# One block for the last three stages, and the ternary weights prepared beside the routed steps

## The reference, cut to what matters

```python
x = x + xattn0(ctx, layernorm(x))       # y * silu(layernorm(x))
x = x + moe0(layernorm(x))              # shared + sum of 4 weighted experts
x = x + xattn1(ctx, layernorm(x))       # y * silu(layernorm(x))
x = x + ffn1(layernorm(x))

def quant_weight(w):
    scale = mean(abs(w)) + 1e-5
    return clip(round(w / scale), -1, 1), scale
def quant_act(x):
    s = max(abs(x), -1) / 127 + 1e-5
    return clip(round(x / s), -128, 127), s
# ffn1: q(silu(q(x) @ wg) * (q(x) @ wu)) @ wd, each product times both scales
```

## Time and profile before

| what | us |
|---|---|
| time, median of 3 (2215.13 to 2220.52) | 2215.22 |
| the profiled execution's own time | 2215.32 |
| its span, first to last instruction | 2213.5 |
| tanh of the last routed slot | 1825.42 |
| first gather of `combine` | 1842.26 |
| first matmul of `quant_ffn` | 2018.26 |

### The profile page before, as it was taken

The page is one execution under the profiler, slowest core; times in us unless marked ns, Lnnn a source line. Parts: engine busy times, 40 slices in busy tenths (PEclk is TensorE's granted clock), DMA queues, the critical chain, the costliest instruction groups (busy, mean ns, idle before and its releaser), DMA issues. The chain is left out here.

```text
span 2213.5 us, 27156 instructions
## 1 busy us (share of the span) xinstructions
PE 1629.5 (74%) x8480; PEld 944.7 (43%) x8502; DVE 1754.3 (79%) x2275; ACT 1160.7 (52%) x1773; POOL 1339.9 (61%) x648
## 2 busy tenths in 40 slices
PE   4475666756638558889888889999999990016998
PEld 1122222212217545666566556665556660003554
DVE  2999999999955847997799758887488885856886
ACT  5676776666633025443544365554555550734776
POOL 2679878789952003995399518886168883752111
PEclk7787988889976579999999999999999995557999
DMA  7546546356442820001000333444434227640000
GB/s 264 192 144 212 178 160 213 128 193 203 171 153 77 161 74 6 11 11 39 10 11 1 127 131 118 167 158 162 156 115 166 79 76 307 178 152 6 20 25 29
DMA packets 127144, 264.63 MB, mean 120 GB/s; under 512 B 44546, under 2 KB 48386, under 8 KB 121794
## 3 DMA queue, kind: packets, MB, share of 16 engines
q1 hardware_dynamic: 93890, 184.24, 24.7%
q0 software_dynamic: 11520, 37.76, 5.7%
q10 hardware_dynamic: 21600, 40.90, 5.0%
HBM read 180.41 MB, written 82.44 MB: 119 GB/s over the span
## 5 line engine op out<-in xcount | busy, mean ns | idle before, releaser
L483 POOL TENSOR_TENSOR ssm_hs<-ssm_hs,ssm_Cs 128x1024 f32<-128x1024 f32 x128 | 314.1, 2463 | 88.3 <-DVE ssm_hs L450 88.3
L483 POOL TENSOR_TENSOR moe_hs<-moe_hs,moe_Cs 128x1024 f32<-128x1024 f32 x128 | 301.5, 2356 | 54.7 <-DVE moe_hs L450 53.6
L450 DVE TENSOR_TENSOR_SCAN moe_hs<-moe_dA,moe_bu 128x1024 f32<-128x1024 f32 x128 | 292.5, 2285 | 21.2 <-ACT moe_dA L364 12.7
L473 POOL TENSOR_TENSOR moe_U<-moe_U,moe_hs 128x1024 f32<-128x1024 f32 x128 | 301.8, 2358 | 6.4
L450 DVE TENSOR_TENSOR_SCAN ssm_hs<-ssm_dA,ssm_bu 128x1024 f32<-128x1024 f32 x128 | 291.6, 2279 | 0.1
L296 PE MATMUL ssm_pY<-ssm_hs,ssm_ident 128*128 128x512 f32 x512 | 272.3, 659 | 4.2 <-POOL ssm_hs L483 4.2
L1246 PE MATMUL moe_pgu<-moe_xsh,all_Wreg 128*128 128x256 f16 x1408 | 248.5, 275 | 1.1 <-DVE moe_hsl L1483 0.8
L1296 PE MATMUL moe_pgu<-all_Wreg,moe_xth 128*128 x1280 | 243.6, 313 | 0.0
L706 POOL TENSOR_TENSOR ssm_wlo<-ssm_wst,ssm_whi 128x1360 f16<-128x1360 f32 x64 | 190.4, 2975 | 44.3 <-ACT ssm_wst L642 44.3
L364 ACT ACTIVATE ssm_dA<-ssm_dlt,ssm_A 128x511 f32<-128x511 f32 x256 | 167.9, 709 | 63.8 <-DVE ssm_hs L450 60.9
L1246 PE MATMUL moe_pgu<-moe_xsl,all_Wreg 128*128 128x256 f16 x704 | 193.7, 275 | 0.0
(11 more groups left out here) (248 smaller groups left out, 3471.9 us busy)
## 6 DMA issues: line engine op xcount, KB each, us to landing
ssm_wst<-in_w_all SPq DMA_DIRECT2D x64, 680.0 KB, 4.9
w_hi<-ssm_whi SPq DMA_DIRECT2D x64, 340.0 KB, 2.3
w_lo<-ssm_wlo SPq DMA_DIRECT2D x64, 340.0 KB, 3.1
y_d<-moe_yo ACTq DMA_DIRECT2D x80, 256.0 KB, 3.1
all_Wreg<-w_hi SPq DMA_DIRECT2D x16, 1088.0 KB, 5.5
all_Wreg<-w_lo SPq DMA_DIRECT2D x16, 1088.0 KB, 8.8
ssm_Cs<-c_d SPq DMA_DIRECT2D x64, 256.0 KB, 5.3
gate_Y<-y_ssm ACTq DMA_DIRECT2D x8, 1024.0 KB, 9.4
```

The lines of the kernel that those rows point to most:

```text
L450: self.nc.vector.tensor_tensor_scan(self.hs[:, j, :, :].rearrange("p k t -> p (k t)"), self.dA[:, q, :, :].rearrange("p k t -> p (k t)"), ...
L473: self.nc.gpsimd.tensor_tensor(Y, Y, self.hs[:, j, :, :], ALU.add).then_inc(self.acc_done, 1)
L483: self.nc.gpsimd.tensor_tensor(self.hs[:, j, :, :], self.hs[:, j, :, :], self.Cs[:, i:i + 1, :].to_broadcast([P, HC, L]), ALU.mult)\
```

## The change

`combine`, `gate(1)` and `quant_ffn` become one block, `tail`. It combines 4 tiles, gates these 4, and starts the feed-forward part on tile 0. The other 12 tiles are combined and gated in between the quarters of the feed-forward tiles (tables `COMBINED`, `GATED`, `FETCHED`, function `gate_at`). There are 16 gather buffers. The root is taken per batch, twice, so that ACT goes from silu's table to the root's and back.

The ternary weights are made in the routed slots by a new class `Ternary`, in 24 pieces of 128x1024 and two passes. Pass 0 (3 of 4 slots from g = 3): load and sum of magnitudes. g = 36: total and scale. Pass 1 (2 of 3 slots from g = 40, so up to g = 75): load again, scale and round up on ACT, clip on POOL, convert on ACT, store to DRAM as bf16. `tail` loads them from there.

```diff
+class Ternary:
+    N = 24
+    ABS, TOTAL, ROUNDS = 3, 36, 40
+    LEAD = 3
+    def job(self, g):
+        for z, first, num, den in ((0, self.ABS, 3, 4), (1, self.ROUNDS, 2, 3)):
+            n = g - first
+            if n >= 0 and (n == 0 or n * num // den > (n - 1) * num // den) and n * num // den < self.N:
+                return z, n * num // den
+        return None
+    def act_abs(self, act, j):
+        act.wait_ge(self.w_in[j % 4], 16 * (j // 4 + 1))
...
+        self.nc.scalar.activation(self.q, self.W[j % 4], ACT.Abs, accum_out=...).then_inc(self.abs_rdy, 1)
+    def act_up(self, act, n):
...
+        self.nc.scalar.activation(w, w, ACT.Identity, bias=self.rnd[:, 0:1],
+                                  scale=self.inv[:, n // 8:n // 8 + 1]).then_inc(self.up_rdy, 1)
+    def pool_clip(self, pool, n):
+        w = self.W[(self.N + n) % 4]
+        pool.wait_ge(self.up_rdy, n + 1)
+        self.nc.gpsimd.tensor_scalar(w, w, ROUND + 1.0, ROUND - 1.0, ALU.min, ALU.max).then_inc(self.clip_rdy, 1)
+    def act_out(self, act, n):
+        act.wait_ge(self.clip_rdy, n + 1)
+        if n:
+            act.wait_ge(self.q_out, 16 * n)
+        self.nc.scalar.activation(self.q, self.W[(self.N + n) % 4], ACT.Identity, bias=self.rnd[:, 1:2])...
+    def pe_total(self, pe):
+        pe.wait_ge(self.tot_rdy, 1)
+        pe.wait_ge(self.set_rdy, 3)
+        self.nc.tensor.matmul(self.px_of()[:, 0, 0:3], self.ones[:], self.tot[:], ...).then_inc(self.all_rdy, 1)
+        pe.wait_ge(self.sc_rdy, 1)
 # experts_and_ssm, POOL
                     if 0 <= g < NSTEP - 2:
                         pool.wait_ge(tx_rdy, g + 1)
                         fetch(g + 2)
+                    if g >= 0 and Q.job(g) and Q.job(g)[0] == 1:
+                        Q.pool_clip(pool, Q.job(g)[1])
 # experts_and_ssm, PE, ahead of x_transpose(g + 1)
+                    if g == Q.TOTAL:
+                        pe.wait_ge(xl_rdy, g + 1)
+                        Q.pe_total(pe)
 # experts_and_ssm, ACT, at the end of the slot
+                    job = Q.job(g) if g >= 0 else None
+                    if g >= 2 and Q.job(g - 2) and Q.job(g - 2)[0] == 1:
+                        Q.act_store(act, Q.job(g - 2)[1])
+                    if g >= 1 and Q.job(g - 1) and Q.job(g - 1)[0] == 1:
+                        Q.act_out(act, Q.job(g - 1)[1])
+                    if job:
+                        z, j = job
+                        if z == 0:
+                            Q.act_abs(act, j)
+                        else:
+                            Q.act_up(act, j)
+                    if job and z * Q.N + j + Q.LEAD < 2 * Q.N:
+                        Q.act_load(act, z * Q.N + j + Q.LEAD)
 # experts_and_ssm, DVE: after h_lo(g - 1) in slot 36
+                    if g == Q.TOTAL:
+                        Q.dve_scale(dve)
-def combine(nc, d, r, X, Wq, wsc):
-def quant_ffn(nc, d, r, X, Wq, wsc, out):
+def tail(nc, d, r, X, y_ssm, out):
+        NR = 16
+        COMBINED = {0: (5, 6, 7), 1: (8,), 2: (9,), 3: (10, 11), 4: (12,), 5: (13,), 6: (14,), 7: (15,)}
+        FETCHED = {0: (9,), 1: (10, 11), 2: (12,), 3: (13,), 4: (14,), 5: (15,)}
+        GATED = {(1, 2): 0, (1, 3): 1, (2, 0): 2, (2, 1): 3}
+        def root_at(b, t, f):
+            return b + 1 < B and (t, f) == ((0, 3) if b == 0 else (0, 1))
 # SP
+                load_y(0)
+                sp.wait_ge(used, 2 * TOPK)
+                for z in range(2):
+                    sp.dma_start(Wq[z][:], r["wq_d"][z]).then_inc(w_in[z], 16)
+                load_y(1)
+                sp.dma_start(Wq[2][:], r["wq_d"][2]).then_inc(w_in[2], 16)
 # POOL
+                for i in range(KC + 1):
+                    fetch(i)
+                for i in range(KC):
+                    y_gate(i)
+                for i in range(KC + 1, 2 * KC + 1):
+                    fetch(i)
 # DVE
+                def combined(i):
+                    dve.wait_ge(used, (i + 1) * TOPK)
+                    V.bn_stats(st[:, 0, i, :], X[:, i, :]).then_inc(c_st, 1)
+                    dve.wait_ge(c_st, i + 1)
+                    V.bn_aggr(mv[:, 0, i, :], st[:, 0, i, :]).then_inc(c_mv, 1)
+                def gated(i):
+                    dve.wait_ge(tr_rdy, i + 1)
+                    V.tensor_tensor(X[:, i, :], X[:, i, :], y_bank(i)..., ALU.add).then_inc(xa_rdy, 1)
+                    dve.wait_ge(xa_rdy, i + 1)
+                    V.bn_stats(st[:, 1, i, :], X[:, i, :]).then_inc(a_st, 1)
+                    dve.wait_ge(a_st, i + 1)
+                    V.bn_aggr(mv[:, 1, i, :], st[:, 1, i, :]).then_inc(a_mv, 1)
+                for i in range(KC):
+                    combine(i)                  # 4 weighted additions, then combined(i)
+                norm(0, 0, c_sd, c_rs, c_ln)
+                combine(KC)
+                for i in range(KC):
+                    gated(i)
+                norm(1, 0, a_sd, a_rs, a_ln)
                 x_scale(0)
+                V.tensor_scalar(xq[:, 0, :], xn[:, 0, :], -ROUND, 127.0, ALU.add, ALU.min).then_inc(xq_rdy, 1)
                 x_scale(1)
 # DVE, behind each quarter f of tile i, b, t = divmod(i, KC)
+                        if len(tiles) == 3:
+                            if f < 3:
+                                combine(tiles[f])
+                        else:
+                            for q in range(f * len(tiles), (f + 1) * len(tiles)):
+                                weighted(tiles[q // TOPK], q % TOPK)
...
+                        if root_at(b, t, f):
+                            norm(0, b + 1, c_sd, c_rs, c_ln)
+                        if b + 1 < B and (t, f) in GATED:
+                            gated((b + 1) * KC + GATED[t, f])
+                        if b + 1 < B and (t, f) == (2, 2):
+                            norm(1, b + 1, a_sd, a_rs, a_ln)
 # ACT, in quarter f
+                        if b + 1 < B and (t, f) == (2, 2):
+                            root(1, b + 1, a_mv, a_sd)      # ahead of the quarter's silu
...
+                        if root_at(b, t, f):
+                            root(0, b + 1, c_mv, c_sd)
+                        for j in gate_at(b, t, f):
+                            gate_of(j)
```

More of the change, by code:

```diff
@@ L1454, in _ @@
                             S.act_z(act, b, 2 * (at - 6) + c)
+                    if g == 1:
+                        act.wait_ge(s_dn, NU)
+                        for j in range(Q.LEAD):
+                            Q.act_load(act, j)
+                    job = Q.job(g) if g >= 0 else None
[11 more added lines that the diff above has]
+                        Q.act_load(act, z * Q.N + j + Q.LEAD)
+                act.wait_ge(Q.q_out, 16 * Q.N)
                 h_hi(NSTEP - 1)
@@ L1732, in _, with fetch, y_gate, x_clip @@
                 sp.wait_ge(o_out, 16 * TT)
+            @block.gpsimd
+            def _(pool):
+                def fetch(i):
+                    for k in range(TOPK):
+                        g = i * TOPK + k
+                        if g >= NR:
+                            pool.wait_ge(used, g - NR + 1)
+                        nc.gpsimd.indirect_dma_start(
+                            out=yr[:, g % NR, :], out_offset=None, in_=r["y_d"],
+                            in_offset=bass.IndirectOffsetOnAxis(ap=r["pos"][:, i, k:k + 1], axis=0)).then_inc(got[g % NR], 16)
+                def y_gate(i):
+                    b, t = divmod(i, KC)
+                    if t == 0:
+                        pool.wait_ge(y_in[b], 16)
+                    pool.wait_ge(g_rdy, i + 1)
+                    y = Y[:, b % 2, t, :]
+                    nc.gpsimd.tensor_tensor(y, y, G[:, b % 2, t, :], ALU.mult).then_inc(yg_rdy, 1)
+                def x_clip(i):
+                    pool.wait_ge(xr_rdy, i + 1)
+                    if i >= 2:
+                        pool.wait_ge(tx_rdy, i - 1)
+                    nc.gpsimd.tensor_scalar(xq[:, i % 2, :], xn[:, i % 2, :], -ROUND, 127.0, ALU.add,
+                                            ALU.min).then_inc(xq_rdy, 1)
+                for i in range(KC + 1):
[4 more added lines that the diff above has]
+                    fetch(i)
+                for i in range(TT):
+                    b, t = divmod(i, KC)
+                    if i + 1 < TT:
+                        x_clip(i + 1)
+                    for f in range(FC):
+                        for j in gate_at(b, t, f):
+                            y_gate(j)
+                    for j in FETCHED.get(i, ()):
+                        fetch(j)
             @block.vector
@@ L1824, in _ @@
                 act.wait_ge(rnd_set, 1)
+                act.wait_ge(eps_rdy, 1)
+                nc.scalar.activation(warm[:], eps[:], ACT.Sqrt)
+                root(0, 0, c_mv, c_sd)
+                for i in range(KC):
+                    gate_of(i)
+                nc.scalar.activation(warm[:], eps[:], ACT.Sqrt)
+                root(1, 0, a_mv, a_sd)
                 layernorm(0)
@@ L1893, in down @@
                     mm.then_inc(dn_rdy, 1)
```

(13 more changed lines are left out.)

308 lines of the change are left out of this document (179 added, 129 removed).

## The result

The changed kernel takes 2235.14 us at the median of 5 runs (2227.8 to 2242.29), the kernel before 2215.22 beside it (2213.64 to 2222.07): ratio 1.0084, 95% interval 1.0065 to 1.0103. It is slower by 0.8%; the forecast was 2258, slower by 1.9%. The sign and the range held, the size was more than twice too large.

A forecast was written before the change was run, and what follows sets the result against it. PE was taken to bound the routed slots and the feed-forward loop. 2215.3 + 102 (routed slots) - 122 (up to the first feed-forward matmul) + 63 (loop) = 2258 us; own range 2238 to 2275, full range 2203 to 2280.

The forecast's parts named there:

- Term 1: Routed slots: cost of making the ternary weights there, 2 + 4 + 7 + 83 + 6 = +102 us.
- 13 + 18.7c: Slots g = 48 to 75: predicted loss in us over 9.3 three-slot periods, for a clip taking c us.
- the circle's 83: Slots g=48 to 75: clip waits for ACT, next gather behind it, PE for that gather; 28.4 for 19.5 us, +83.
- the entry: At g = 48: the clip comes ahead of `pool_y_init`, which must wait for that slot's tanh; +6 us.
- the clip is cheap: Rival, POOL's queue in g = 48 to 75: below 1.4 us per clip the change is faster; chance 0.20.
- Term 2: From the first gather after the routed slots to the first feed-forward matmul: 53.5 us in place of 176.0, 122 saved.
- Term 3: Feed-forward loop: additions, gates, norms moved onto DVE and table loads make it 249 for 184.5 us, +63.
- additions fit: Rival, feed-forward loop: the additions fit into DVE's waits, +25 in place of +63, time 2220; chance 0.10.
- three table stalls: Loop, quarter (2, 2) of three batches: root ahead of silu with table loads idles DVE 3.6 us each, 11 together.
- No circle: Rival, routed slots: only POOL's own work counts, 25.0 us for three slots, +51 in place of +83, 2226; chance 0.12.
- PE's clock falls: Rival, routed slots: sparser slots lower PE's clock, +7 (2265), or +41 (2299) at 1.2 GHz throughout; chance 0.08.

The follow-up runs named there:

- a dear clip: Changed kernel with POOL's clip replaced by addition and minimum, f32 to bf16 into an unread tile, pieces stored unclipped: 2264.09 us, ratio 1.0221.
- the two steps together: Changed kernel with the clip, conversion and store one slot later, loads two jobs ahead, and the store right behind the conversion: 2189.9 us, ratio 0.9901.

## Why the prediction was wrong in size

**Term 1, +102 forecast, +64.8 measured: the step that failed is the price of the clip, 3.74 for 1.06, worth 50 us too much; a second one hid half of that.** The prediction said "I take 3.74, since it is the same operation". It was the same instruction with another pair of operations, and the pair sets the price: 1.06. The doubts it named, one input and a bf16 output, were the right worry with a wrong reason, for the output's type has no part in it. The rule quoted from the Trainium skill (GPSIMD Engine Reference, Engine selection), one input at roughly line rate, gave an estimated 0.9 and holds for minimum and maximum (1.04 to 1.09), roughly as the page says; addition with minimum contradicts it at 3.66.

By the prediction's own formula, 13 + 18.7c, the right price makes 33 of the circle's 83; measured are 59.3 (27 intervals, 235.0 against 175.8). So the rest was off the other way by 26. With the right price and nothing else changed the prediction's sum would be 2208, faster than before: that the sign held is luck, two errors partly cancelled. Of the 26, 6.6 belong to the entry: the slot from g = 50 to 51 takes 13.16, because the gather that POOL issues behind its work of g = 48 and 49 starts 14.3 later than before (that slot takes 12.42 without the clips, so they are not its only cause). That leaves 52.6 in 26 intervals. At c = 3.66 the formula is right within 0.2 for three slots; at 1.06 it gives 23.07, and 25.6 came. The runs show why in part. With a dear clip the turn closes as I wrote it, through POOL's second clip slot. With a cheap one POOL comes to its clip early and the turn closes through the first gather and one slot of PE instead: by my legs about as long, 1.1 + 4.8 + 4.1 + 4.44 + 6.51 + 1.7 = 22.7. In the turn shown, 2.1 more for a landing and 2.2 more for the lowered clock are added, which is that turn's whole excess. It is an extreme one: the median landing is 3.8. Prices in the same place: slots of 6.51 before, 7.26 without a clip, 8.71 at 1.06, 9.48 and 9.52 at 3.66. More is lost with the wait of a cheap clip than with its dearer work.

One term that the prediction put at nothing is not nothing: it cost loads and stores at nothing, "hidden behind some 26 us of lead". The loads have that lead; the store has none, since the next conversion waits for it (20.7 us in nine places). In the changed kernel it is covered, as moving the store alone gains nothing; once the clip stands later, the store's place is worth 21 us.

The rival *the clip is cheap* had the price right and still missed by its threshold: it decides "at c = 1.4", and at 1.06 the change is slower.

The small terms: pass 0 costs +0.6 from g = 0 to 35 (242.6 for 242.0), and 0.3 to 3.1 in the other ten traces, which leaves room for the forecast's +2; the scale at g = 36 costs 5.3, not 4; the passes in g = 40 to 47 cost 1.4, not 7; the entry, forecast at +6, is +5.4, as g = 48 to 51 took 24.4 before and 29.8 after. With 52.6, and a first routed tanh 0.6 earlier, these make the 64.8 but for rounding.

**Term 2, -122 forecast, -120.4 measured**, 55.6 against 53.5 for the head. Right, with small errors that cancel: the last of the 16 gathers is in use at 32.3 where 28.9 was forecast, and from there it took 23.2 in place of 24.6.

**Term 3, +63 forecast, +67.4 measured.** The mechanism, DVE setting the tiles that carry additions, was right: 0.82 an addition, nine tenths of it visible, the last five tiles at PE's 11.52, and DVE waits only 28.9 us for the silus. The rival *additions fit* is out. The 11 us that I set down for three table stalls are not shown: ACT's waits are there (4.5 at the longest, 11.8 in three), but taking them away gave 0.3. So the term's sum is near and one of its parts is misplaced. The added drain from the Trainium skill (ScalarE: Activation LUTs, What ACT_TABLE_LOAD costs) is again not in the trace: root 1.29 behind the start of a load of 1.28.

**The rivals.** *No circle* is refuted by the two steps together: POOL's work is the same there, and the slots fall from 8.71 to 7.01, though its time (2226) lay nearer than mine. *PE's clock falls* was right as a side effect: 0.93 in the routed slots for 1.00, and a part of the 26.

Altogether, on the spans: forecast +43, measured +12.5; term 1 is off by -37.2, the others by +6.8. What stays open: how the roughly 20 us that the cheap clip's circle takes beyond its formula divide between late landings and the clock, and what holds the best version at 7.01 instead of 6.51 in a slot.

## What to carry to other kernels

Take the price of an instruction from a row with the same operations, not just the same opcode; where no such row exists, one run of both forms is cheaper than any argument. A wait of an in-order queue for work of the same slot closes a circle through all engines. Here it cost 39 us with an instruction of 1.06 us behind it, and 60 with one of 3.66: move the instruction one slot later before making it faster. When two waits stand side by side, undoing one can show nothing: here one gave 24 us, the other none, both 45. Undo both before either is called harmless.

## What the hardware showed that I had not expected

POOL's TENSOR_SCALAR of 128x1024 with minimum and maximum takes 1.04 to 1.09 us at the mean of a group, with addition and minimum 3.64 to 3.70, whether it writes f32 or bf16. A weighted DVE addition (SCALAR_TENSOR_TENSOR) of 16 columns from SBUF takes 284 ns at the mean and 225 at the least, where 512 columns take 817 at the mean. In one turn, after some 5 us without matmuls in slots that were otherwise dense, the granted clock was 0.50 for 4 us and 0.92 for the next 2.7, and the same transposition and `up` took 6.61 instead of 4.44.
